# Group norm: mean folded into the value weights, inverse root on 64 columns, a new order of steps

## What is computed

```python
def step(s, rkvw):
    r_t, k_t, v_t, w_t = rkvw
    a = k_t[:, :, :, None] * v_t[:, :, None, :]
    out = jnp.einsum('bhk,bhkd->bhd', r_t, u * a + s)
    return (a + w_t[:, :, :, None] * s, out)
...
m = jnp.mean(a4, axis=-1, keepdims=True)
var = jnp.mean((a4 - m) ** 2, axis=-1, keepdims=True)
att = ((a4 - m) * jax.lax.rsqrt(var + EPS)).reshape(b, l, E) * gn_w + gn_b
x = x + att * g @ Wo.T
```

## Time and profile before

| | us |
|---|---|
| median of 3 runs | 2381.81 (2381.59 to 2382.89) |
| profiled execution, its own time | 2377.0 |
| its span, first to last instruction | 2375.0 |
| TensorE busy | 2211.8 (93%) |
| VectorE busy | 2137.8 (90%) |
| ScalarE busy | 1020.3 (43%) |
| GpSimd busy | 600.2 (25%) |

### The profile page before, as it was taken

One profiled execution on the slowest core, in us unless ns is written; L12 is line 12 of the kernel. 1 busy time (PEld: TensorE's weight loads), 2 busy tenths in 40 slices (PEclk: granted clock), 3 DMA queues, 4 the chain that ended last, 5 costly groups with the idle time before them and its releaser, 6 DMA issues. The chain is left out here.

```text
span 2375.0 us, 41883 instructions
## 1 busy us (share of the span) xinstructions
PE 2211.8 (93%) x14272; PEld 1528.4 (64%) x14272; DVE 2137.8 (90%) x5337; ACT 1020.3 (43%) x3265; POOL 600.2 (25%) x858
## 2 busy tenths in 40 slices
PE   4697999999999999999999999999999999999866
PEld 3374766767676676767667676766767676666533
DVE  1369999999999999999999999999999999999973
ACT  2535263544526254452635345363634536363101
POOL 1122214131222404122241412223141232314200
PEclk8798999999999999999999999999999999999977
DMA  7001001010010101001010100101010010100000
GB/s 263 21 10 31 1 11 39 1 48 2 10 39 11 39 1 49 2 10 39 11 39 1 49 1 15 35 11 39 1 49 1 19 31 10 39 2 28 1 18 9
DMA packets 48420, 61.61 MB, mean 26 GB/s; under 512 B 20209, under 2 KB 25969, under 8 KB 48209
## 3 DMA queue, kind: packets, MB, share of 16 engines
q1 hardware_dynamic: 48208, 58.93, 7.9%
HBM read 42.14 MB, written 16.78 MB: 25 GB/s over the span
## 5 line engine op out<-in xcount | busy, mean ns | idle before, releaser
L1149 DVE TENSOR_TENSOR_SCAN st<-ws,st 128x256 f32<-128x256 f32 x1024 | 653.6, 702 | 0.2
L846 ACT ACTIVATE probs_or_mixes<-probs_or_mixes,least 128x128 f32<-128x128 f32 x1024 | 396.9, 396 | 105.8 <-DVE least L1096 105.6
L1000 POOL COPY st<-s 128x8 f32<-128x8 f32 x256 | 67.0, 279 | 1097.6 <-issue 933.7
L1138 DVE TENSOR_TENSOR st<-bank_pair,kT 128x1016 f32<-128x1016 f32 x256 | 308.8, 1206 | 29.4 <-PE bank_pair L696 21.7
L1159 DVE TENSOR_TENSOR st<-st,rT 128x1024 f32<-128x1024 f32 x256 | 329.4, 1302 | 0.0
L1096 DVE CUSTOM_DVE_ANT_0 probs_or_mixes<-bank,nmask 128x128 f32<-128x128 f32 x1024 | 228.8, 285 | 66.2 <-POOL nmask L988 33.8
L1024 POOL TENSOR_TENSOR probs_or_mixes<-probs_or_mixes 128x512 f32<-128x512 f32 x160 | 200.0, 1278 | 133.2 <-DVE probs_or_mixes L1215 133.2
L1030 POOL TENSOR_TENSOR rstd<-rstd,mhalf 128x1 f32<-128x1 f32 x96 | 95.0, 989 | 416.0 <-DVE rstd L1180 416.0
L846 ACT ACTIVATION_READ_ACCUMULATOR probs_or_mixes<-probs_or_mixes,least 128x1 f32 x1024 | 199.1, 194 | 0.0
L696 PE MATMUL bank_pair<-v_hi,sel 32*128 32x256 f32 x1024 | 165.7, 333 | 12.5 <-DVE st L1138 12.3
L857 ACT ACTIVATE probs_or_mixes<-bank 128x512 f32<-128x512 f32 x256 | 141.7, 594 | 78.6 <-PE bank L571 74.3
(11 more groups left out here) (139 smaller groups left out, 4207.9 us busy)
## 6 DMA issues: line engine op xcount, KB each, us to landing
cin<-in_ctx SPq DMA_DIRECT2D x16, 512.0 KB, 3.7
...
```

Source lines behind the costliest of these rows:

```text
L846: last = fn(pr[:, n % 4, j, :], pr[:, n % 4, j, :], ACT.Exp, bias=least[:, n, j:j + 1], scale=-1.0, accum_out=rsum[:, n, j:j + 1])
L1138: tt(dst, src, over(kv, DU, 1), ALU.mult).then_inc(outer.sem, 1)
L1149: last = nc.vector.tensor_tensor_scan(v, ws[:, c].rearrange("p b t -> p (b t)"), v, 0.0, ALU.mult, ALU.add)
```

## The change

- `mean` and its two passes on ScalarE are gone. The value weights are multiplied by `centre` once, at the first `low`, in 16 products of 128 columns (`centre_value_weights`), into `bank7` and `pair`, and copied by ScalarE into `big["wvv"]`. They are loaded as rows, into the buffers of `kT` and `gT`; `headb`, `centre` and `meanb` lie in that of `rT`.
- A step `state` on ScalarE takes the mean off the first state, chunk by chunk, and `first` waits for it.
- `square` reads `att` itself. `var` is cut into four quarters of 64 columns (`TQ`), which land in different eights of the same 32 partitions: 16 products in place of 4. The inverse root works on 128 x 64.
- `rstd` is one step of 16 products, with 32 rows of weights, 64 columns; each half has two chunks at a time, in two banks, and the second half waits for the first.
- All four orders are written anew. `reduce.4`, `spread.12` and, on ScalarE, `turn_n` and `low` stand at the beginning of the next pass.

Not shown of the diff: POOL_ORDER, the declarations of semaphores, the smaller load of `gn_row` and that of `headb` and `meanb`.

```diff
 PE_ORDER = """
-low_rank.0+1 reduce.5+2 spread.13+2 turn_c.0 turn_c.1 mean.0+2 tdecay.0+1 spread.14+2 low_rank.2+1 proj_r.0+1
-spread.15+2 decay.0+1 turn_x.0 proj_v.0+1 proj_k.0+1 key.0 reduce.6+2 spread.0+1 decay.1+1 turn_x.1 reduce.7+2
-low_rank.4+1 spread.1+1 proj_r.1+1 query.0 spread.2+1 mean.1+2 score.0 var.0+2 query.1 proj_g.0+1 spread.3+1 rstd.0+2
-rstd.1+2 proj_g.1+1 score.2 reduce.0+1 spread.4+1 value.0 turn_p.0 turn_p.1 turn_p.2 spread.5+1 score.4 score.6
-out.0+2 turn_p.3 reduce.1+1 values.0 spread.6+1 out.1+2 turn_p.4 score.8 spread.7+1 turn_p.5 turn_p.6 proj_v.1+1
-turn_p.7 proj_k.1+1 turn_m.0+2 score.10 flip.0 values.1 turn_p.8 turn_p.9 share.0 spread.8+1 score.12 turn_p.10
-reduce.2+1 score.14 turn_p.11 project.0 turn_m.1+2 turn_p.12 turn_p.13 values.2 reduce.3+1 flip.1 turn_p.14 turn_p.15
-spread.9+1 share.1 values.3 ffn_k.0+2 spread.10+1 project.1 ffn_k.1+2 ffn_r.0+2 spread.11+1 ffn_r.1+2 turn_n.0
-turn_n.1 ffn_v.0+2 ffn_v.1+2 low.0 reduce.4+1 spread.12+1
+reduce.4+2 spread.12+2 low_rank.0+1 turn_c.0 spread.13+2 reduce.5+2 tdecay.0+1 spread.14+2 turn_c.1 low_rank.2+1
+proj_r.0+1 turn_x.0 decay.0+1 spread.15+2 proj_v.0+1 proj_k.0+1 turn_x.1 key.0 reduce.6+2 spread.0+1 decay.1+1
+low_rank.4+1 spread.1+1 reduce.7+2 query.0 spread.2+1 var.0+2 proj_r.1+1 spread.3+1 score.0 query.1 rstd.0+2
+proj_g.0+1 spread.4+1 score.2 proj_g.1+1 reduce.0+1 value.0 turn_p.0 turn_p.1 turn_p.2 score.4 score.6 spread.5+1
+turn_p.3 out.0+2 values.0 reduce.1+1 turn_p.4 out.1+2 turn_p.5 spread.6+1 turn_p.6 score.8 turn_p.7 proj_v.1+1
+proj_k.1+1 score.10 spread.7+1 flip.0 values.1 turn_p.8 turn_p.9 turn_p.10 spread.8+1 share.0 score.12 score.14
+reduce.2+1 turn_p.11 project.0 turn_m.0+2 values.2 turn_m.1+2 spread.9+1 turn_p.12 turn_p.13 flip.1 turn_p.14
+turn_p.15 reduce.3+1 share.1 values.3 ffn_k.0+2 project.1 spread.10+1 ffn_r.0+2 ffn_k.1+2 spread.11+1 ffn_r.1+2
+turn_n.0 turn_n.1 ffn_v.0+2 ffn_v.1+2 low.0
 """
...
 ACT_ORDER = """
-turn_c.0 turn_c.1 mean.0+2 tdecay.0+1 proj_r.0+1 proj_v.0+1 turn_x.0 decay.0+1 key.0 proj_k.0+1 decay.1+1 turn_x.1
-proj_r.1+1 query.0 mean.1+2 score.0 query.1 proj_g.0+1 proj_g.1+1 score.1 score.2 turn_p.0 turn_p.1 turn_p.2 score.3
-score.4 turn_p.3 score.5 score.6 score.7 turn_p.4 score.8 turn_p.5 proj_v.1+1 turn_p.6 turn_p.7 apply2.0+2 apply2.1+2
-score.9 proj_k.1+1 turn_m.0+2 flip.0 score.10 turn_p.8 turn_p.9 share.0 score.11 turn_p.10 score.12 score.13
-turn_p.11 score.14 score.15 turn_m.1+2 turn_p.12 turn_p.13 flip.1 turn_p.14 turn_p.15 share.1 apply0.0 ffn_k.0+2
-apply0.1 apply1.0 ffn_k.1+2 apply1.1 ffn_r.0+2 turn_n.0 turn_n.1 ffn_r.1+2 low.0
+turn_n.0+1 turn_n.1+1 low.0+1 state.0+1 turn_c.0 tdecay.0+1 turn_c.1 turn_x.0 proj_r.0+1 decay.0+1 square.0+2
+state.1+1 proj_v.0+1 proj_k.0+1 key.0 turn_x.1 decay.1+1 square.1+2 query.0 proj_r.1+1 score.0 query.1 state.2+1
+score.1 proj_g.0+1 proj_g.1+1 score.2 turn_p.0 turn_p.1 turn_p.2 score.3 score.4 turn_p.3 score.5 score.6 turn_p.4
+score.7 state.3+1 turn_p.5 turn_p.6 score.8 turn_p.7 proj_v.1+1 score.9 proj_k.1+1 score.10 turn_p.8 turn_p.9 flip.0
+apply2.0+2 turn_p.10 apply2.1+2 share.0 score.11 score.12 score.13 score.14 turn_p.11 score.15 turn_m.0+2 turn_m.1+2
+turn_p.12 turn_p.13 flip.1 turn_p.14 turn_p.15 share.1 apply0.0 ffn_k.0+2 apply0.1 ffn_k.1+2 apply1.0 ffn_r.0+2
+apply1.1 ffn_r.1+2
 """
...
 DVE_ORDER = """
-weigh.12+2 outer.15+2 scan.13+2 scan.14+2 scan.15+2 proj_v.0+1 weigh.13+2 weigh.14+2 weigh.15+2 outer.0+1 row2.0+2
-scan.0+1 mix.4+1 key.0 outer.1+1 keep_row.0 readout.3+2 scan.1+1 weigh.0+1 weigh.1+1 outer.2+1 score.0 score.1
-var.0+2 scan.2+1 outer.3+1 groupnorm.0+2 proj_g.0+1 scan.3+1 proj_g.1+1 score.2 outer.4+1 score.3 value.0 scan.4+1
-score.4 weigh.2+1 score.5 weigh.3+1 outer.5+1 score.6 score.7 out.0+2 scan.5+1 norm2.0+2 outer.6+1 out.1+2 score.8
-norm2.1+2 weigh.4+1 score.9 weigh.5+1 inverse.0 scan.6+1 proj_v.1+1 outer.7+1 weigh.6+1 score.10 score.11 readout.0+1
-scan.7+1 score.12 score.13 gather.0 outer.8+1 score.14 score.15 scan.8+1 weigh.7+1 project.0 inverse.1 shift2.0+2
-norm0.0 outer.9+1 gather.1 scan.9+1 project.1 norm0.1 weigh.8+1 norm1.0 readout.1+1 outer.10+1 weigh.9+1 norm1.1
-outer.11+1 scan.10+1 row1.0 scan.11+1 shift.0 ffn_v.0+2 weigh.10+1 ffn_v.1+2 weigh.11+1 outer.12+1 mix.0 mix.1
-readout.2+1 outer.13+1 scan.12+1 mix.2 outer.14+1 mix.3
+outer.15+2 scan.14+2 scan.15+2 weigh.13+2 weigh.14+2 proj_v.0+1 weigh.15+2 outer.0+1 scan.0+1 weigh.0+1 outer.1+1
+readout.3+2 row2.0+2 mix.4+1 outer.2+1 var.0+2 scan.1+1 score.0 score.1 outer.3+1 weigh.1+1 groupnorm.0+2 scan.2+1
+score.2 proj_g.0+1 scan.3+1 proj_g.1+1 score.3 outer.4+1 value.0 scan.4+1 score.4 score.5 score.6 key.0 weigh.2+1
+weigh.3+1 outer.5+1 score.7 out.0+2 scan.5+1 norm2.0+2 weigh.4+1 out.1+2 inverse.0 outer.6+1 norm2.1+2 score.8
+readout.0+1 weigh.5+1 score.9 proj_v.1+1 scan.6+1 score.10 outer.7+1 score.11 weigh.6+1 scan.7+1 score.12 gather.0
+score.13 weigh.7+1 score.14 outer.8+1 score.15 scan.8+1 project.0 inverse.1 norm0.0 shift2.0+2 gather.1 outer.9+1
+weigh.8+1 scan.9+1 project.1 norm0.1 row1.0 weigh.9+1 outer.10+1 keep_row.0 norm1.0 readout.1+1 norm1.1 outer.11+1
+scan.10+1 scan.11+1 shift.0 weigh.10+1 ffn_v.0+2 weigh.11+1 ffn_v.1+2 outer.12+1 mix.0 mix.1 outer.13+1 readout.2+1
+scan.12+1 mix.2 mix.3 outer.14+1 weigh.12+1 scan.13+1
 """
...
-        consts = sb("consts", [P + P + P + 2 + 56])
-        ident, meanb, headb = consts[:, 0:P], consts[:, P:2 * P], consts[:, 2 * P:3 * P]
-        centre = headb
-        parity, ebase = consts[:, 3 * P:3 * P + 2], consts[:, 3 * P + 2:3 * P + 58]
+        consts = sb("consts", [P + 2 + 56 + 56])
+        ident, parity = consts[:, 0:P], consts[:, P:P + 2]
+        ebase, mbase = consts[:, P + 2:P + 58], consts[:, P + 58:P + 114]
...
+        headb, centre, meanb = rT[:, 0, 0:P], rT[:, 0, P:2 * P], rT[:, 1, 0:P]
+        wv_rows = [t[:].rearrange("p c n -> p (c n)").rearrange("p (c n) -> p c n", c=2) for t in (kT, gT)]
...
+        spare = [bank[7][:], pair[:, 0], pair[:, 1], bank[7][:]]
...
+            for half in range(2):
+                wload(2, wv_rows[half], w["wvv"][half * T:half * T + T].rearrange("(c p) n -> p c n", p=P))
...
+            def centre_value_weights():
+                for e in range(NC):
+                    if e == 3:
+                        pe.wait_ge(centred_v, 1)
+                    for c in range(NC):
+                        last = mm(spare[e][:, c * P:(c + 1) * P], wv_rows[c // 2][:, c % 2, e * P:(e + 1) * P], centre,
+                                  start=True, stop=True)
+                    last.then_inc(turned_v, 1)
...
-            def mean(g, p):
-                pe.wait_ge(emptied[XB.of(("readout", 2 * p + 1))], XB.through(("readout", 2 * p + 1), g))
-                ps, full = y_bank(("mean", p), g)
-                for q in range(2):
-                    last = mm(ps[:, q * T:(q + 1) * T], centre, att[:, 2 * p + q, :], start=True, stop=True)
-                last.then_inc(full, 1)
-
             def var(g, _):
                 pe.wait_ge(squared.sem, squared.after(g, 2))
                 ps, full = y_bank(("var", 0), g)
-                for c in range(NC):
-                    last = mm(ps[32 * c:32 * c + 32, 0:T], meanb[:, 0:32], sq[:, c, :], start=True, stop=True)
-                last.then_inc(full, 1)
-
-            def spread_rstd(g, p):
+                for q in range(4):
+                    o = 24 - 8 * q
+                    for c in range(NC):
+                        last = mm(ps[32 * c:32 * c + 32, 0:TQ], mbase[:, o:o + 32], sq[:, c, q * TQ:(q + 1) * TQ],
+                                  start=q == 0, stop=q == 3)
+                last.then_inc(full, 1)
+            def spread_rstd(g, _):
                 pe.wait_ge(newton.sem, newton.after(g, 11))
-                ps, full = y_bank(("rstd", p), g)
-                for q in range(2):
-                    last = mm(ps[:, q * T:(q + 1) * T], bsel[:, 2 * p + q, :], y, start=True, stop=True)
-                last.then_inc(full, 1)
+                ps = [y_bank(("rstd", p), g) for p in range(2)]
+                for m in range(2):
+                    if m == 1:
+                        pe.wait_ge(half_rstd.sem, half_rstd.after(g, 2))
+                    for q in range(4):
+                        for c in (m, m + 2):
+                            o = m * T + q * TQ
+                            last = mm(ps[c // 2][0][:, o:o + TQ], bsel[32 * c:32 * c + 32, q, :],
+                                      y[32 * c:32 * c + 32, :], start=True, stop=True)
+                            if q == 3:
+                                last.then_inc(half_rstd.sem if m == 0 else ps[c // 2][1], 1)
...
+                if first_group(g):
+                    for e in range(NC):
+                        act.wait_ge(turned_v, e + 1)
+                        fn(big["wvv"][:, e, :], spare[e], ACT.Copy).then_inc(centred_v, 1)
...
-            def mean(g, p):
```

(25 more changed lines are left out.)

42 lines of the change are left out of this document (27 added, 15 removed).

## The result

The changed kernel takes 2405.3 us (median of 4 runs, 2401.5 to 2408.6) against 2381.7 (4 runs) before: a ratio of 1.0107 [1.0093, 1.0121]. It is slower by 24 us where the forecast said faster by 24, and outside the range. The profiled execution took 2408.4 us with a span of 2406.4; the mean granted clock of the span is 0.957, where before it was 0.969.

The account below looks back on a forecast made before the run. TensorE and VectorE, waiting for each other, were taken as the bound. A period of 136.3 us, -1.43, gave -20.0 over 14 periods; with edges -3.3, that is -23.3, from 2381.8 to 2358 us, range 2335 to 2372, chance 0.49.

Parts of the forecast that it names:

- The bound and the term of VectorE: TensorE and VectorE bind together, waiting for each other; VectorE's own work per period falls from 133.21 to 131.0 us.
- TensorE's own terms: TensorE's work per period: mean -1.73, rstd +0.11 and +0.30, var +0.10, shape changes +0.66; sum -0.56 us, 134.89 to 134.33.
- rival 2: In rstd the two weight loads of a pair run serially: +1.95 instead of +0.11 us, total 2384; chance 0.09.
- rival 4: Short instructions in var and rstd each carry an unhidden fixed cost, 0.86 us on 48 more, total 2371; chance 0.08.
- Newton: VectorE's inverse-root operations on 64 columns take 2.9 instead of 5.14 us, -2.2 a period.
- ScalarE: Four state steps add at most 6 us, mean copies go; ScalarE ends at 68 of 136 us and bounds nobody.
- third rival: A ScalarE state step, state.3 ahead of turn_p.5, delays an evacuation TensorE needs: up to 1.5 us a period, 2390; chance 0.17.
- The changes of tile shape: TensorE's switches between whole, row and column tiles rise from 54 to 58 a period, costing +0.66 us.
- The edges: Start and end of the run: last chain -4.1 us, value-weight products at the start +3; -3.3 us with Newton in pass 16.
- rival 1: Only TensorE's work counts and its stalls stay at 2.87 us a period: -11 us, 2371; chance 0.17.
- The stalls: TensorE's waits per period fall from 2.87 to 2.0 us as the 1.1 us turn_n stall nearly vanishes; four others stay.
- The clock: TensorE's granted clock was read at its upper level, 2.4 GHz, between first and last slices; no term was given for it.

Follow-up runs that it names:

- e5: Kernel before, its orders and mean steps kept, with only the inverse root changed to 64 columns: 2364.1 us, 0.9943 of before.
- e6: Mean off the value weights and first state alone, inverse root on 256 columns, in the orders of before: 2367.1 us, 0.9949 of before.
- e9: e1 with three spread steps each moved ahead of a transpose on TensorE, 58 tile-shape changes instead of 52: 2370.9 us, 0.9968 of before.
- e1: The changed computation in the orders of the kernel before, mean steps left out, square and state steps put in: 2353.1 us, 0.9896 of before.
- e2: The changed kernel with ScalarE's evacuation of share.0 moved ahead of both apply2 steps: 2382.5 us, 1.0020 of before.
- e4: The changed kernel with both edits, share.0 evacuated before apply2 and turn_x.1 moved between decay.1 and low_rank.4: 2397.8 us, 1.0080 of before.
- e7: e1 with TensorE's stretch at share.0 ordered as in the changed kernel, share.0 still evacuated early on ScalarE: 2371.2 us, 0.9974 of before.
- e3: The changed kernel with turn_x.1, four whole-array transposes, moved between decay.1 and low_rank.4: 2411.1 us, 1.0145 of before.
- e11: The changed kernel with the share.0 stretch set nearly back to the order of before on TensorE and ScalarE: 2425.4 us, 1.0191 of before.

## Why the prediction was wrong, step by step

**The bound and the term of VectorE: right.** Its busy time is 131.38 us in the pass from 984.01 and 130.08 in the clean one, forecast 131.0. e5 and e6 show either engine's saving to be paid in part, as was argued.

**TensorE's own terms: right, on a base a little off.** The period read in the earlier trace rows does not run from `var` to `var`, and it lies in a stretch where passes are 138.1 us long: its 134.89 and 2.87 are 135.24 and 2.52 in the pass from 976.14, whose L615 stall is 0.8 us and not 1.1. From like pass to like pass TensorE goes from 135.24 to 134.68, which is the -0.56 of the forecast. The new steps in the clean pass of after, with the start of the next, as the earlier trace rows show the old ones:

```profile
846.11 0.65 PE L758 MATMUL bank<-last_stage,consts 128*32 128x64 f32 x32
846.70 2.64 PE L702 MATMUL bank<-probs_or_mixes,wr 128*128 128x256 f32 x11
...
855.53 2.31 PE L772 MATMUL bank<-last_stage,bsel 32*128 32x64 f32 x32
857.76 1.99 PE L702 MATMUL bank<-probs_or_mixes,wg 128*128 128x256 f32 x8
```

`var` takes 0.59 us for 32 short instructions, +0.02 (forecast +0.10). `rstd` takes 2.23, +0.40 with the wait for its first half (forecast +0.11 +0.30); a pair starts 0.112 us after the one before. So rival 2 (0.23 a pair) and rival 4 are out. A round of four in `var` takes 0.056 us, below the 0.06 that was the mark; by the Trainium skill, "TensorEngine Tiling (Array Packing)", Performance Considerations, each matmul has some 60 cycles of overhead, which as an estimate would be 0.6 us on the 24 more instructions of `var`; the rows show 0.02.

**Newton: right.** From 985.97 to 989.12, 3.15 us against 5.14, so -2.0 (forecast -2.2). An operation takes 0.23 and has 0.03 to the next:

```profile
985.97 0.21 DVE L1292 TENSOR_SCALAR last_stage<-bank 128x64 f32<-128x64 f32 x1
...
989.12 1.27 DVE L1194 TENSOR_TENSOR_SCAN st<-ws,st 128x256 f32<-128x256 f32 x2
```

**ScalarE: right in sum.** 66.3 to 66.8 us a pass (forecast 68). By form (busy us, mean ns, idle before), the two parts of `state` and the square:

```profile
L985 ACT ACTIVATE s<-s,less_s 128x16 f32<-128x16 f32 x128 | 32.4, 300 | 2.1
L981 ACT ACTIVATE junk<-s 128x16 f32<-128x16 f32 x128 | 25.9, 204 | 1.9
L981 ACT ACTIVATION_READ_ACCUMULATOR junk<-s 128x1 f32 x128 | 24.2, 189 | 0.0
L975 ACT ACTIVATE last_stage<-att 128x512 f32<-128x512 f32 x32 | 19.9, 622 | 107.5 <-DVE att L1214 107.5
```

No `state` step holds TensorE up in the passes read; the third rival's step was the wrong one.

**The changes of tile shape: right in number, a little small.** 58 in the trace as counted from the string; 0.21 us each in e9, against the 0.17 taken. Four cost 0.85 by that, as an estimate, not 0.66 (which the forecast's own prices, three at 0.2 and one at 0.12, would have made 0.72).

**The edges: right in the parts that were named.** The last chain, from the last chunk of `att` to `out`, went from 15.4 us (2313.03 to 2328.42 before) to 12.0 (2347.99 to 2359.96), -3.4 where -4.1 was forecast. The 32 instructions at the start take 4.95 us, not 7, because the clock rises in their midst (four instructions in 0.85 us at first, in 0.45 later). The last stretch holds more than the chain, though: from the last but two `var` to the end after takes 303.4 us (from 2102.98) and before 296.2 (from 2078.77), since the last of the 14 passes lasts 140.87 us in after, with falls of the clock, and 133.05 in before; no term of the forecast stands for that. In e1 the span is 2351.5, -23.5 against before; the forecast's sum was -23.3. But the sum is right there by two errors that cancel: e1 has 52 changes of shape and not 58, so TensorE is at 133.21 and not at 134.33, and its stalls are 3.3 us and not 2.0. That is rival 1's view of the stalls, in a kernel with less work than was forecast.

**The stalls: the step that failed.** "The other four I leave as they are, since VectorE's slack helps them and new neighbours hurt. 2.87 goes to 2.0." The `turn_n` stall did go. But the four orders were written anew, and none of the new neighbours was followed. TensorE misses 3.22 us in the clean pass of after, where 2.0 was forecast and the like pass of before has 2.52. With the work as forecast, this alone eats the gain: 137.90 for 137.76. The largest new stall is the mechanism of the third rival, "a step on ScalarE holds back an evacuation that TensorE waits for", at a place that it did not name, and not with a `state` step: `apply2.0`, `turn_p.10` and `apply2.1` ahead of `share.0`, all of which stood in the diff. The place named in "what would show it", VectorE waiting at `groupnorm` for `rstd`, is there with 1.2 us (0.3 in e1), where VectorE has 7.8 us of the pass to spare. The stalls at `share.0` matter through the clock: taking them away gained nothing in a clean pass (e2).

**The clock: the other step that failed.** It was noted as at its upper level throughout the middle and taken as given for the new order. The new order lost 1.97 us a pass, some 28 us over 14 passes, to falls that no pass of before had. Before ran similar steps at this place without one: `share`, `spread`, a stall of 0.26 us, `score`, then the transposes of `turn_p.10` on the whole array:

```profile
887.47 1.13 PE L562 MATMUL bank<-kbd,inputs_turned 32*128 32x256 f32 x8 [0.26 <-ACT probs_or_mixes L857]
888.53 0.66 PE L571 MATMUL bank<-consts,probs_or_mixes 128*128 128x128 f32 x4
```

Without the falls after would be at about 137.9 a pass, as an estimate some 28 us less, 2378: level with before. So the gain was lost to the stalls, and the slower time is the clock's. The ends of the range, 2335 and 2372, were no help: stalls of 1.2 to 2.4 give 2347 to 2364 by the forecast's own sum, and no rival had a term for the clock.

**What stays open.** Which mixture of part-array steps and idle time brings a fall. e2, e4 and e7 differ from their neighbours by one or two swaps and have falls in 4, 6 and 6 passes; e3, e4 and e11 show falls staying or coming at another place when one is mended. Within one execution passes with the same steps and stalls fall or don't: 3 passes of after have the stall of 1.05 us without a fall, and the wait of 1.1 us for L1260 comes with falls in some passes of e6, e7 and e9 and in none of e1. No rule that fits all thirteen kernels was found, so the price of a fall is shown here (1.6 us for one of 3.4, from 137.90 to 139.48), and that e1 has none is an observation, not a forecast. Left untraced too is the 0.55 us of the budget.
